# Feed-forward part of a cross-attention block: token halves in the two row halves, sixteen units of 256 columns

## What is computed

```
x = x + attention(layernorm(x), ctx)      # q and k normalised per head, softmax, @ Wo
z = layernorm(x)
s = z @ Win + bin_                        # [tokens, 64]
h = relu(s[..., None] * W1 + b1)          # [tokens, 64, 16], W1 and b1 are [64, 16]
g = sum_h(h * W2) + b2                    # [tokens, 64]
x = x + g @ Wout + bout
```

## Time and profile before

| | |
|---|---|
| median of 3 runs | 485.91 us (485.61 to 488.14) |
| profiled execution, its own time | 485.37 us |
| its span, first to last instruction | 483.6 us |
| busy: PE, DVE, ACT, POOL | 446.4, 367.9, 317.8, 205.4 us |
| mean granted clock of TensorE | 0.968 of full speed |
| chain that ended last | PE 72%, DVE 14%, ACT 4%, issue 4% |

### The profile page before, as it was taken

One profiled execution on the slowest core, in us unless ns is written; L12 is line 12 of the kernel. 1 busy time (PEld: TensorE's weight loads), 2 busy tenths in 40 slices (PEclk: granted clock), 3 DMA queues, 4 the chain that ended last, 5 costly groups with the idle time before them and its releaser, 6 DMA issues.

```text
span 483.6 us, 7610 instructions
## 1 busy us (share of the span) xinstructions
PE 446.4 (92%) x2392; PEld 299.4 (62%) x2392; DVE 367.9 (76%) x710; ACT 317.8 (66%) x571; POOL 205.4 (42%) x191
## 2 busy tenths in 40 slices
PE   5999889999999999999999999999969997998865
PEld 2466667466578737774677567865745663486643
DVE  4897785677868996799688977786978557477965
ACT  5559738878738883797469754985397359734551
POOL 3327786156344452545252522744435240425310
PEclk9999979999999999999999999999998998998977
DMA  8543883953931195318541593019513860430003
GB/s 308 149 142 105 199 204 86 195 136 65 238 90 46 48 279 121 80 44 224 147 111 45 130 240 67 4 45 238 121 37 117 187 134 1 152 111 0 0 36 139
DMA packets 25207, 58.32 MB, mean 121 GB/s; under 512 B 5840, under 2 KB 6352, under 8 KB 22096
## 3 DMA queue, kind: packets, MB, share of 16 engines
q1 hardware_dynamic: 20304, 49.18, 40.7%
q10 hardware_dynamic: 4864, 8.65, 5.2%
HBM read 22.17 MB, written 8.39 MB: 63 GB/s over the span
## 4 chain that ended last, share of the span: by engine, by line
PE 72%; DVE 14%; ACT 4%; issue 4%; SPq 4%; DMA 1%; DVEq 0%; ACTq 0%
PE bank L1857 41%; PE bank L1863 9%; PE bank L1956 7%; PE bank L1944 6%; PE bank L1922 4%; PE bank L1959 2%; DVE mx L739 2%; DVE ssq L727 2%; DVE bank L817 2%; DVE ln L635 2%; ACT hid L1383 1%; DMA xin<-in_x_dram 1%; PE bank L1968 1%; DVE ln L638 1%; PE bank L1988 1%
## 5 line engine op out<-in xcount | busy, mean ns | idle before, releaser
L739 DVE TENSOR_REDUCE mx<-bank 128x4 f32<-128x512 f32 x128 | 83.1, 685 | 26.4 <-PE bank L1922 26.1
L1305 ACT ACTIVATE prob<-bank 128x512 f32<-128x512 f32 x128 | 72.6, 599 | 28.6 <-PE bank L1944 26.1
L489 POOL TENSOR_TENSOR qt_lo<-u,qt_hi 128x512 fp32r<-128x512 f32 x32 | 41.3, 1290 | 72.5 <-ACT u L1282 72.2
L1956 PE MATMUL bank<-prob,v_kv 128*32 128x512 f32 x256 | 65.7, 614 | 0.2
L1959 PE MATMUL bank<-prob,den_sel 128*32 128x512 f32 x256 | 65.2, 614 | 0.0
L503 POOL TENSOR_TENSOR x<-x,bout_row 128x512 f32<-128x512 f32 x28 | 35.9, 1286 | 63.9 <-DVE bn L778 37.9
L1857 PE MATMUL bank<-wq_hi,zt_hi 128*128 128x512 f32 x128 | 54.3, 424 | 1.9 <-DVE prob L676 1.2
L1857 PE MATMUL bank<-wq_lo,zt_hi 128*128 128x512 f32 x128 | 51.1, 399 | 0.0
L1857 PE MATMUL bank<-wq_hi,zt_lo 128*128 128x512 f32 x128 | 51.0, 398 | 0.0
L494 POOL TENSOR_TENSOR at_lo<-att,at_hi 128x512 fp32r<-128x512 f32 x28 | 35.5, 1287 | 36.0 <-ACT at_hi L1356 36.0
L1383 ACT ACTIVATE hid<-s_in,b_col,w_col 128x512 f32<-128x512 f32 x64 | 47.6, 808 | 2.4 <-DVE s_in L797 2.2
(11 more groups left out here) (170 smaller groups left out, 995.3 us busy)
## 6 DMA issues: line engine op xcount, KB each, us to landing
q_stack<-qt_hi SPq DMA_DIRECT2D x64, 256.0 KB, 4.7
xin<-in_x_dram SPq DMA_DIRECT2D x36, 256.0 KB, 2.9
q_stack<-qt_lo SPq DMA_DIRECT2D x32, 256.0 KB, 4.7
x<-in_x_dram SPq DMA_DIRECT2D x28, 256.0 KB, 4.7
out_dram<-x ACTq DMA_DIRECT2D x28, 256.0 KB, 4.0
att<-in_L_xattn_Wk_dram SPq DMA_DIRECT2D x1, 1024.0 KB, 6.5
x<-in_L_xattn_Wq_dram SPq DMA_DIRECT2D x4, 256.0 KB, 7.5
hid<-in_L_xattn_Wv_dram SPq DMA_DIRECT2D x1, 1024.0 KB, 10.3
```

Of the source, the lines that this page charges most:

```text
L489: pool.tensor_tensor(qt_lo[:, :, cols], u[:, j, :].rearrange("p (i n) -> p i n", i=HC), qt_hi[:, :, cols].bitcast(F32), ALU.subtract).then ...
L739: dve.tensor_reduce(mx[:, j, :].rearrange("p (g i) -> p i g", g=G)[:, 2 * half:2 * half + 2, 2 * r:2 * r + 2], maxs_banks[T][half][j][r][: ...
L1305: act.activation(prob[:, h % PR, :], score_bank[t][h][:, :], ACT.Exp, scale=SCALE).then_inc(exp_done, 1)
L1956: pe.matmul(at_bank[t][c][rows(n), :], v_kv[kv_of(t)][:, n * HD:(n + 1) * HD], prob[:, n % PR, :], start=True, stop=True)
```

## The change

The two halves of the partitions no longer hold two halves of the hidden units, but two halves of a block's tokens: tiles 0 and 1 above, 2 and 3 below. Each has all sixteen units.

- `z2_high` and `z2_low` become one copy, `z2_move`, in float32, into the buffer of the hidden units (`hid`; for the last block `prob`). It waits until the hidden sums of the block before are done.
- `project_s` is float32: eight matmuls of 256 columns that write 64 partitions each, alternately the upper and the lower half. `win_hi` and `win_lo` go, with the steps that made them.
- `spread_rstd` is four float32 matmuls with 64 output partitions in place of four transposes of 128.
- `move_rstd`, `scale_s`, `hidden`, `add_hidden`, `g_high` and `g_low` work on 256 columns; there are sixteen hidden units a block, and `hid` has room for eight.
- `project_y` is called for two token columns `j`; each call makes three matmuls for the upper 64 rows and three for the lower, alternating, into the banks of tiles j and 2 + j. `residual2` and `store` take the tiles in the order 0, 2, 1, 3.
- Every table of banks and the order lists of all engines are new. The stores stay on ScalarE.

```diff
-HH = INNER // 2
+HH = INNER
+HT = TB // 2
-RR = 4
+RR = 8
-        win_hi = sb("win_hi", [P, C, 2, M], F32R)
-        win_lo = sb("win_lo", [P, C, 2, M], F32R)
+        win = sb("win", [P, C, M])
-        hid = sb("hid", [P, RR, TOK])
+        hid = sb("hid", [P, RR, HT * P])
-        y_bank = banks_of([(0, 5, 6, 0)] * 4 + [(0, 4, 5, 0)] + [(1, 7, 4, 1)] + [(0, 7, 7, 4)] + [(6, 3, 6, 0)])
+        y_bank = banks_of([(2, 7, 4, 3)] * 4 + [(5, 6, 2, 7)] + [(7, 6, 0, 5)] + [(0, 4, 2, 0)] + [(7, 4, 2, 7)])
...
+        def z2t_of(T):
+            return prob[:, :, :] if last(T) else hid[:, :, :].rearrange("p (c a) n -> p c (a n)", a=2)
+        def of_half(a):
+            return a[:, 0:HT * P]
+        def place(j):
+            return 2 * (j % HT) + j // HT
...
-            def z2_low(T, j):
-                cols = slice(j * P, (j + 1) * P)
-                dve.wait_ge(z2t_hi_done, T * TB + j + 1)
-                dve.tensor_tensor(z2t_lo_of(T)[:, :, cols], z2_bank[T][j][:, :].rearrange("p (c n) -> p c n", c=C),
-                                  z2t_hi_of(T)[:, :, cols].bitcast(F32), ALU.subtract).then_inc(z2t_lo_done, 1)
...
-                dve.tensor_tensor(s_in[:, :], s_bank[T][:, :], s_in[:, :], ALU.mult).then_inc(s_done, 1)
+                dve.tensor_tensor(of_half(s_in), of_half(s_bank[T]), of_half(s_in), ALU.mult).then_inc(s_done, 1)
...
-                    dve.scalar_tensor_tensor(out=s_bank[T][:, :], in0=hid[:, hh % RR, :], scalar=w2_col[:, hh:hh + 1],
-                                             in1=s_bank[T][:, :], op0=ALU.mult, op1=ALU.add).then_inc(hsum_done, 1)
+                    dve.scalar_tensor_tensor(out=of_half(s_bank[T]), in0=hid[:, hh % RR, :], scalar=w2_col[:, hh:hh + 1],
+                                             in1=of_half(s_bank[T]), op0=ALU.mult, op1=ALU.add).then_inc(hsum_done, 1)
...
+            def z2_move(T, j):
+                act.wait_ge(z2_turned, T * TB + j + 1)
+                if last(T):
+                    act.wait_ge(pv_done, BLOCKS * PAIRS)
+                elif first(T):
+                    act.wait_ge(kv_projected[1], NB)
+                else:
+                    act.wait_ge(hsum_done, T * HH)
+                act.activation(z2t_of(T)[:, :, j * P:(j + 1) * P], z2_bank[T][j][:, :].rearrange("p (c n) -> p c n", c=C),
+                               ACT.Copy).then_inc(z2t_done, 1)
...
-                act.activation(hid[:, hh % RR, :], s_in[:, :], ACT.Relu, bias=b1_col[:, hh:hh + 1],
+                act.activation(hid[:, hh % RR, :], of_half(s_in), ACT.Relu, bias=b1_col[:, hh:hh + 1],
                                scale=w1_col[:, hh:hh + 1]).then_inc(hid_done, 1)
...
-                for j in range(TB):
-                    ins = pe.transpose(rstd_bank[T][:, j * P:(j + 1) * P], ln2[:, 3, j:j + 1].broadcast_to([P, P]), ident[:, :])
+                for j in range(HT):
+                    for half in range(2):
+                        ins = pe.matmul(rstd_bank[T][M * half:M * (half + 1), j * P:(j + 1) * P],
+                                        ln2[:, 3, HT * half + j:HT * half + j + 1].broadcast_to([P, M]), ident[:, :],
+                                        start=True, stop=True)
...
-                three_pass(s_bank[T][:, :], [(both(win_hi, c), both(win_lo, c), z2t_hi_of(T)[:, c, :], z2t_lo_of(T)[:, c, :])
-                                         for c in range(C)]).then_inc(s_mm_done, 1)
+                for c in range(C):
+                    for half in range(2):
+                        ins = pe.matmul(of_half(s_bank[T][M * half:M * (half + 1), :]), win[:, c, :],
+                                        z2t_of(T)[:, c, HT * P * half:HT * P * (half + 1)], start=c == 0,
+                                        stop=c == C - 1)
...
-                three_pass(y_bank[T][j][:, :], [(at_hi_of(T)[:, 0, cols], at_lo_of(T)[:, 0, cols], wout_hi[:, :],
-                                                 wout_lo[:, :])]).then_inc(y_done, 1)
+                g_hi, g_lo = at_hi_of(T)[:, 0, cols], at_lo_of(T)[:, 0, cols]
+                for n, (g, w) in enumerate(((g_hi, wout_hi), (g_hi, wout_lo), (g_lo, wout_hi))):
+                    for half in range(2):
+                        rows = slice(M * half, M * (half + 1))
+                        ins = pe.matmul(y_bank[T][HT * half + j][:, :], g[rows, :], w[rows, :], start=n == 0, stop=n == 2)
+                ins.then_inc(y_done, 1)
```

More of the change, by code:

```diff
@@ L2459, in epilogue @@
[L2459 to L2463 removed]
+                pe.wait_ge(mx_done[0], 60)
+                scores(6, 5)
+                pe.wait_ge(qf_done, 31)
+                turn_q(7, 3)
+                spread(5, 3)
+                pe.wait_ge(exp_done, 101)
+                scores(6, 6)
+                pe.wait_ge(exp_done, 102)
+                pe.wait_ge(att_done, 23)
@@ new lines, in epilogue @@
+                project_y(4, 0)
+                pe.wait_ge(att_done, 24)
+                pe.wait_ge(g_done, 5)
+                project_y(4, 1)
+                pe.wait_ge(qf_done, 32)
+                scores(6, 7)
+                pe.wait_ge(out_done, 17)
+                values(6, 2)
+                pe.wait_ge(out_done, 18)
+                scores(6, 8)
+                pe.wait_ge(exp_done, 103)
+                scores(6, 9)
+                pe.wait_ge(exp_done, 104)
+                scores(6, 10)
```

1741 lines of the change are left out of this document (880 added, 861 removed).

## The result

The changed kernel takes 480.82 us (median of 4 runs, 480.54 to 481.64); the kernel before took 485.76 beside it. The ratio is 0.989, 95% interval 0.986 to 0.993: 4.9 us or 1.1% faster, where 15.6 us were forecast. The profiled execution took 480.67 us, its span is 478.9 us.

A forecast was written before the change was run, and what follows sets the result against it. TensorE was taken to bound the loop, a chain through VectorE, ScalarE and TensorE the end. 10.5 us (blocks 0 to 6) plus 5.1 (end) gave 15.6 off 485.37: 469.8, forecast 470, range 462 to 484.

The forecast's parts named there:

- TensorE's gain, 2.1 us a block: TensorE, each block: project_s 1.03 less, project_y 1.25 less, minus 0.2; bounds -1.2 and 2.3 us.
- The 0.2 for the change of form: TensorE, ahead of project_s and project_y: 0.2 us a block laid on for changing to the tiled form.
- The wait for g, 0.6 us: Ahead of project_y: g ready 18.5 us after project_s, TensorE's own work 17.9, so it stands 0.6 us; bounds nothing and 3.8.
- Net gain a block 1.5 us: TensorE's 2.1 less the 0.6 us wait, laid on blocks 0 to 6 (four loop, three epilogue): 10.5 us.
- other waits of the new order: Sign of a wrong forecast: waits, such as for shared banks, ahead of TensorE for over a microsecond a repeat.
- VectorE's 43.40 busy us: Loop: VectorE's busy time in one 51.83 us repeat before the change, against TensorE's 51.16, ScalarE's 37.27.
- ScalarE rises to about 39 of 50 us and has room: ScalarE, each block: sixteen units at 0.50 cost 8.0 against 5.6 us, three smaller copies save 0.4.
- The middle, forecast 4.5 us shorter: Middle of the epilogue, scale_s(3) to scale_s(6): three blocks, 4.5 us less.
- The end, 5.1 us: End of the run: the last block's chain 3.1 us less, block 6's first two steps 2.0 less.
- The price of a dependent add: VectorE: a 256-column add waiting for the one before costs 0.585 us; in the last block sixteen cost 2.5 more.
- Both terms of TensorE: Last block: project_s 4.59 to 2.95 us, 1.6 less; project_y 4.61 to 2.4, 2.2 less.
- the gain that goes into the wait for g (481 us): Rival, 20%: g comes 2.1 us or more late, TensorE's saving turns idle, only the end's 5.1 us remains: 480.3.

The follow-up runs named there:

- e2: The change with half of the sixteen hidden units left out on ScalarE and VectorE in every block, orders kept: 470.48 us, 0.966 of the kernel before.
- e15: The change with one wait added in GpSimd's loop order, att_low(t-2, 1) starting only after newton1(t+2): 474.67 us, 0.977 of the kernel before.
- e16: The kernel before with one wait added in GpSimd's loop order, att_low starting only after newton1: 485.39 us, ratio 0.998.
- e3: The change with half of the hidden units left out on ScalarE and VectorE in blocks 4 to 7 alone: 469.81 us, 0.967 of the kernel before.
- e4: The change with ScalarE computing eight hidden units in blocks 4 to 7 while VectorE still adds sixteen: 480.29 us, 0.988 of the kernel before.
- e6: The change with VectorE adding only eight of ScalarE's sixteen units in blocks 4 to 7: 474.49 us, 0.977 of the kernel before.
- e9: The change with other banks for the last two project_y and all but one of their waits for residual2 gone: 479.45 us, 0.985 of the kernel before.
- e12: The change with GpSimd's late adds of bout (blocks 6 and 7) waiting until the same block's newton2 is through: 480.01 us, 0.987 of the kernel before.
- e7: The change with the sixteen terms of blocks 4 to 7 added into two sums in turn, odd ones in SBUF: 479.60 us, 0.986 of the kernel before.
- e1: The change with project_s and project_y matmuls ordered all of one half, then all of the other: 486.68 us, 1.001 of the kernel before.

## Why the prediction was wrong, and where it was right

- **TensorE's gain, 2.1 us a block: right for the two steps**, 2.07. project_s 1.83 (1.85 forecast), spread_rstd 0.49 (0.46). project_y took 1.86, not 1.63; in e2, where g and the exponentials come early, it takes 1.59, so 0.27 of it is waiting. The 0.2 for the change of form does not stand in these two steps; the next point has more of it.
- **The wait for g, 0.6 us: it was not there.** From scale_s (203.3) to g_low (220.9) it is 17.6 us, and TensorE idles less than 0.2 us ahead of project_y. In its place scores and max_scores cost 0.6 us a repeat more, a term that the forecast put at nothing. So each repaired alike, the change gives 1.4 us a repeat (e15 and e16), near the 1.5 that was forecast, and that is luck: two errors of one size.
- **"Net gain a block 1.5 us", laid on blocks 0 to 6: the step that failed.** In the loop it came to 0.76 as measured. Of the 1.3 us between that and 2.07, 0.6 is what GpSimd's operations cost the new order (1.2 us a repeat, e15) beyond what they cost the old one (0.55, e16), and 0.6 the dearer scores and max_scores. The prediction named the possibility ("other waits of the new order ... in front of TensorE for more than a microsecond a repeat"), but costed these at nothing and never looked at what stands ahead of row_max in VectorE's queue. VectorE's 43.40 busy us were taken as work; 1.9 us of them were two operations of newton1 waiting for GpSimd (1.21 and 0.97 us in the trace of before), which could be read there. The new order has the same stall, and twice as much of it reaches TensorE; that its row_max stands nearer behind newton1 is the likely reason.
- **"ScalarE rises to about 39 of 50 us and has room": right in the loop (38.71), wrong in the epilogue.** There ScalarE and VectorE set the pace together, and the sixteen units and sums cost 7.4 us against eight. The middle, forecast 4.5 us shorter, became 0.7 longer. A share of busy time in the loop was carried over to a stage with another limit. All repairs together regain 2.2 us of the middle; about 3 us of the forecast stay lost there. ScalarE's units and the adds share them (e3, e4, e6); part may be TensorE's clock. Over the whole stage it was granted at 0.94, against 0.95 before, but at 0.70 against 0.79 in 16 us of it (windows below), and no run separated that.

```profile
356.00:372.00 16.00, 12.19 (x51) 5.41 (x51) 14.03 (x28) 14.79 (x30) 7.32 (x8) 0.70 0.00 0
```

```profile
353.00:369.00 16.00, 10.95 (x49) 7.64 (x47) 14.89 (x23) 15.00 (x24) 7.98 (x7) 0.79 0.01 2
```

  The first row is the change's, the second that of the kernel before around the same scale_s(4), which starts at 356.3 and 355.0; in both ScalarE is busy for 15 of 16 us, and TensorE for 12 and 11.
- **The end, 5.1 us: 3.2 came.** The price of a dependent add was right (0.59 for 0.585). Both terms of TensorE were mis-sized by its clock, which the forecast took over from before, where it was granted at 0.63 in both steps. project_s of block 7 ran at 1.00 and took 1.95 us, not 2.95. project_y ran at 0.50: 3.3 us and 0.87 between the calls for 2.4, so of its 2.2 us only 4.61 - 4.2 = 0.4 came. Left out were block 6's adds ahead of scale_s(7) (0.4 us), the bank that two tiles share (1.2 us in e9) and GpSimd's part in newton2 (1.0 in e12).
- **Sum.** The forecast of 470 us is what the kernel takes once three things beside the two steps are mended, GpSimd's timing, the chain of sums and the shared banks (470.05), by gains of other sizes: the loop gives 6.0, not 4.5, the middle 1.5 and not 4.5. That the totals meet is chance. Of the rivals, the gain that goes into the wait for g (481 us) came nearest in time, by another wait than it named.

## What to carry to other kernels

Read each engine's short operations for durations far above their shortest before taking its busy time as work: a four-value operation of 1.2 us is a wait in disguise, and one wait on the engine that causes it gave 6.1 us where 2 us a block of saved matmuls had given 4.9. Repair both kernels before saying what a change is worth: it was 0.8 us a repeat as measured and 1.4 repaired alike. When orders are made anew, look at what stands ahead of every operation that the bound engine waits for. A term from the steady loop holds for the loop; the epilogue, where other engines bound, wants its own sum, above all when the number of small operations doubles.

## What the hardware showed that was not expected

- Some VectorE operations on SBUF wait until GpSimd's running operation is through, and the profile shows the wait as their duration: of the change's small normalising operations (0.15 to 0.20 us else), all 11 that last over 0.9 us behind 80 us end within 30 ns of the end of one of GpSimd's; with GpSimd held back they fall to 0.16 us (e12, e15). row_max and the adds of hidden units, which read a bank, and the sums of squares and the statistics, which read one SBUF tile, kept their lengths beside it (0.68, 0.48, 0.68 and 0.69 us). The Trainium skill ("SBUF — State Buffer", SBUF: two separate sides) has this rule: the two engines share a port pair under an exclusive lock that is held for the whole instruction, and VectorE takes it for two SBUF inputs or in its two-port mode. The traces agree, also in e7, where adds of two SBUF tiles last 1.09 and 1.14 us beside GpSimd and 0.48 else; nothing in the forecast used it.
- TensorE starts matmuls of the other tile ahead of those that stand in front of them in its order: in e1 the first matmul of the second row tile starts 10 ns after the first and 295 ns before the second of the other tile, and of project_s's sixteen records in column tiles four pairs overlapped. The Trainium skill ("TensorE: Matmul & The Clock Gate", Part 3, The mechanism) says that matmuls start in program order. e1's rows differ, so here the measurement decides: alternating the tiles in the code is worth 0.9 us a block for the column tiles and nothing for the row tiles.
